# A graph network's GATv2 layer: its feed-forward node work moved from a phase of its own into the edge sweep, with logits and scatter in column parts

## The reference

```
h  = relu(layernorm(x))
xl = h @ W_l + b_l ; xr = h @ W_r + b_r ; ee = edge_attr @ W_e
m  = leaky_relu(xl[src] + xr[dst] + ee, 0.2)          # one row of 128 per edge
logits = einsum('eho,ho->eh', m, att)                 # 8 per edge
ex = exp(logits - segment_max(logits, dst)[dst])
out = segment_sum(xl[src] * ex / segment_sum(ex)[dst], dst) + b_att
hh  = layernorm(out + h) * g1 + be1
ff  = gelu(hh @ W1 + b1) @ W2 + b2                    # 128 -> 512 -> 128
x   = x + layernorm(hh + ff) * g2 + be2
```

## Time and profile before

| what | value |
|---|---|
| time, median of three runs | 7462.92 us |
| span of the profiled execution | 5796.6 us |
| profiled execution's own time | none is given beside the span; median less span is 1666.3 us |
| GATv2 sweep, first to last gather | 2282.0 to 3349.9 us |
| FFN phase, first operation to the next sweep's first gather | 3407.5 to 3621.1 us |
| PE, DVE, ACT, POOL busy over the span | 79%, 47%, 21%, 69% |

### The profile page before, as it was taken

One profiled execution on the slowest core, in us unless ns is written; L12 is line 12 of the kernel. 1 busy time (PEld: TensorE's weight loads), 2 busy tenths in 40 slices (PEclk: granted clock), 3 DMA queues, 4 the chain that ended last, 5 costly groups with the idle time before them and its releaser, 6 DMA issues. The chain is left out here.

```text
span 5796.6 us, 89863 instructions
## 1 busy us (share of the span) xinstructions
PE 4596.1 (79%) x21959; PEld 3153.3 (54%) x21959; DVE 2702.8 (47%) x8105; ACT 1216.6 (21%) x3182; POOL 3988.9 (69%) x4207
## 2 busy tenths in 40 slices
PE   5888888657777776999999977687777758887887
PEld 4777777535556564444444433455555535555555
DVE  4222222321111113677777766555555545555555
ACT  2111111221211211222222258111111111111111
POOL 6777777457777775777777700777777747777775
PEclk9999999975555555999999989666666666666665
DMA  5333333244444443555555510455555534444443
GB/s 151 106 105 105 105 104 104 74 150 106 112 114 107 118 114 90 160 165 165 165 165 164 166 38 24 109 114 114 113 114 115 113 77 107 111 109 110 109 111 78
DMA packets 559823, 663.58 MB, mean 114 GB/s; under 512 B 196431, under 2 KB 390909, under 8 KB 558717
## 3 DMA queue, kind: packets, MB, share of 16 engines
q1 hardware_dynamic: 424909, 382.99, 22.2%
q0 software_dynamic: 134640, 277.80, 21.1%
HBM read 580.95 MB, written 86.19 MB: 115 GB/s over the span
## 5 line engine op out<-in xcount | busy, mean ns | idle before, releaser
L1792 POOL DMA_INDIRECT soft_rows<-table,sources x2496 | 2388.6, 957 | 1128.2 <-issue 737.7
L1422 POOL DMA_INDIRECT sum_rows<-table,sources x832 | 785.7, 944 | 343.9 <-issue 249.6
L1088 POOL DMA_INDIRECT term_rows<-table,sources x832 | 791.4, 951 | 289.4 <-issue 289.4
L1923 PE MATMUL psum<-soft_onehot,soft_message 128*128 128x64 f32 x3328 | 647.6, 358 | 107.1 <-DVE soft_message L2066 105.0
L1923 PEld LDWEIGHTS psum<-soft_onehot,soft_message 128*128 128x128 f32 x3328 | 586.1, 266 | 188.0 <-issue 181.8
L1119 PE MATMUL psum<-term_onehot,term_term 128*128 128x64 f32 x1664 | 403.9, 425 | 188.5 <-DVE sums L1171 176.6
L1464 PE MATMUL psum<-sum_onehot,sum_rows 128*128 128x64 f32 x1664 | 360.4, 391 | 222.7 <-DMA sum_rows<-table,sources 218.4
L1119 PEld LDWEIGHTS psum<-term_onehot,term_term 128*128 128x128 f32 x1664 | 370.7, 328 | 242.1 <-issue 242.0
L1165 DVE TENSOR_TENSOR term_term<-psum,term_rows 128x512 f32<-128x512 f32 x208 | 143.9, 692 | 753.0 <-issue 349.0
L1464 PEld LDWEIGHTS psum<-sum_onehot,sum_rows 128*128 128x128 f32 x1664 | 343.5, 304 | 278.0 <-issue 273.8
L1919 PEld LDWEIGHTS psum<-soft_onehot,soft_weights 128*4 128x4 f32 (+1 forms) x3328 | 284.9, 109 | 305.9 <-issue 293.0
(11 more groups left out here) (277 smaller groups left out, 6619.9 us busy)
## 6 DMA issues: line engine op xcount, KB each, us to landing
soft_onehotT<-onehotsT SPq DMA_DIRECT2D x312, 256.0 KB
soft_onehot<-onehots SPq DMA_DIRECT2D x624, 128.0 KB, 2.1
soft_attrs<-in_ea128T SPq DMA_DIRECT2D x208, 256.0 KB
soft_rows<-table,sources POOLq DMA_INDIRECT x2496
term_attrs<-in_ea64T SPq DMA_DIRECT2D x208, 128.0 KB, 2.8
onehots<-term_onehot SPq DMA_DIRECT2D x208, 128.0 KB
sum_onehot<-onehots SPq DMA_DIRECT2D x208, 128.0 KB, 2.7
onehotsT<-sum_flat SPq DMA_DIRECT2D x208, 128.0 KB
```

The source lines that it names most:

```text
L1088: pool.indirect_dma_start(rows[:, k, t, :], None, io.table0[0:NCH * CN], bass.IndirectOffsetOnAxis(sb.sources[:, g * TPG + t:g * TPG + t + ...
L1422: pool.indirect_dma_start(rows[:, k, t, :], None, io.table1[0:NCH * CN], bass.IndirectOffsetOnAxis(sb.sources[:, g * TPG + t:g * TPG + t + ...
L1792: pool.indirect_dma_start(rows[:, k, t, :], None, table[0:NCH * CN], bass.IndirectOffsetOnAxis(sb.sources[:, g * TPG + t:g * TPG + t + 1], ...
L1923: last = pe.matmul(bank[:, 0:W], message[:, g.slot(4), b, :], onehot[:, k, b], start=b == 0, stop=b == TPG - 1)
```

## The change

The order of phases becomes first phase, two sweeps with their norms, `gatv2_sweep`, `soft_sweep(3)`, `soft_sweep(4)`; `ffn_phase` is no longer called and `soft_sweep` loses its `full` branches. In `gatv2_sweep`:

- The FFN work (`FfnNodes`, with three `ChunkNorm`) runs inside the sweep in chunks of 256 nodes. It has one PSUM bank (bank 4), which each stage takes over when the one before it is read. Stages are placed by offsets from 2 to 24. The gain and bias of the first norm are applied on ACT in feature-major form. Many of its tiles lie in SBUF of weights that are no longer needed.
- Logits: a whole batch at once at the start of a step, with one attention matrix `att_cols` (128 x 32). Four matmuls write 32 lanes each, on four column quarters of one bank of 128 lanes. The lanes of a batch now fill 128 partitions instead of 32, in one bank instead of two.
- Scatter: the tiles of a group go alternately to rows 0 to 63 and 64 to 127 of the window bank. `flip_window` follows directly and is a matmul with `fold` (two identities on top of each other), which adds the two parts. The weights' transposes become matmuls with `quad_pick`.
- `z` has four buffers instead of two; the starts and continuation masks of a batch are loaded with four DMAs each instead of one.
- 64 steps are unrolled ahead of the loop instead of 16, and the sweep runs on to step 248, where the last chunk is stored.
- The first phase loads five more small constants.

```diff
@@ class FfnNodes: stages (new) @@
+    def act_steps(self, act, t):
+        node_steps(act, t, (2, self.stage), (4, self.norm1.take_root), (6, self.normalise1), (7, self.scaled1), (8, self.gelus(0)), (9, self.gelus(1)),
+                   (12, self.copy_res), (13, self.norm2.take_root), (14, self.normalise2), (19, self.norm3.take_root), (20, self.normalise3),
+                   (21, self.copy_h), (22, self.rows_out))
...
+    def attention(self, v, c, t):
...
+        v.tensor_scalar(self.den, self.dens, 1e-16, None, ALU.add).then_inc(s.den[k], 1)
...
+        v.tensor_tensor(heads, heads, self.den.unsqueeze(3).broadcast_to([P, CB, 8, D // 8]), ALU.mult).then_inc(s.ratio[k], 1)
...
+        self.norm1.statistics(v, c, kept)
@@ def gatv2_sweep: PE (new) @@
+                def head_logits(g):
+                    pe.wait_ge(s.leaky, g.times(1, BATCH))
+                    if g.back(BATCH).exists():
+                        pe.wait_ge(s.factor_log, g.back(BATCH).uses(BATCH))
+                    settle(pe)
+                    for j in range(BATCH):
+                        last = pe.matmul(lane_bank[j * QUAD:(j + 1) * QUAD], sb.att_cols, z[:, j], start=True, stop=True)
...
+                    for b in range(TPG):
+                        last = pe.matmul(window_bank[b % 2 * W:b % 2 * W + W], onehot[:, k, b], message[:, g.slot(2), b, :], start=b < 2, stop=b >= TPG - 2)
...
+                def flip_window(g):
+                    pe.wait_ge(s.window_copied, g.times(1, 1))
...
+                    pe.matmul(window_T[:, 0:W], window[:, 0:D], fold, start=True, stop=True)
...
+                def step(t):
+                    if t.back(BATCH).closes(0):
+                        head_logits(t.back(BATCH))
+                    if t.exists():
+                        edge_terms(t)
+                    nodes.pe_steps(pe, t)
...
+                    g = t.back(LAG)
+                    if g.exists():
+                        scatter(g)
+                        flip_window(g)
@@ def gatv2_sweep: DVE (new) @@
+                def step(t):
+                    g = t.back(1)
+                    if g.exists():
+                        v.wait_ge(s.z, g.times(1, 1))
+                        v.scalar_tensor_tensor(z[:, g.slot(BATCH)], z[:, g.slot(BATCH)], 0.2, z[:, g.slot(BATCH)], ALU.mult, ALU.max).then_inc(s.leaky, 1)
...
+                    if t.exists():
+                        edge_sum(t)
+                    nodes.dve_steps(v, t)
```

More of the change, by code:

```diff
@@ L42 @@
 BATCH = 4
+QUAD = P // BATCH
 LAG = BATCH + 3
@@ L1651, in soft_sweep @@
 def soft_sweep(nc, io, sb, layer):
-    H = {2: 8, 3: 4, 4: 1}[layer]
+    H = {3: 4, 4: 1}[layer]
     L, W = H * BATCH, NARROW
[L1655 to L1658, removed]
+    table, width = {3: (io.table3, D + 4), 4: (io.table4, D + 1)}[layer]
+    dst_table, dst_width = {3: (io.adst3, 4), 4: (io.adst4, 2)}[layer]
@@ L1659, in soft_sweep @@
+    spread = {3: sb.lane_expand4, 4: sb.ones}[layer]
     mask, heads = sb.lane_mask[0:L], sb.lane_head[0:L, 0:H]
     AHEAD = 4
-    DST = AHEAD if full else BATCH
     phase = f"soft{layer}"
[L1663 to L1667, removed]
@@ L1668, in soft_sweep @@
-    s = sems(nc, phase, *names, gathered=AROUND, attr=AHEAD, dst_rows=DST, onehotT=4, onehot=4)
+    FIRST = 4 * AROUND
+    LAST = STEPS * (NCH - 1 + BEHIND) + 14
+    names = ("order cleared starts_in cont_in edge_term leaky src_out logits lanes_out running backward fend carry_psum carry shift init_psum init maxima "
+             "shifted factor_log weights_lane factor spread weights_T weights_out factor_psum factor_out message "
+             "scattered").split()
+    s = sems(nc, phase, *names, gathered=AROUND, dst_rows=BATCH, onehotT=4, onehot=4)
@@ L1711, in soft_sweep @@
         factor_head_bank = sb.psum[0:H, 7, 48:48 + BATCH]
-        nodes = None if full else GatNodes(nc, io, sb, tile, layer, sb.psum[:, 2, :])
-        CLEARED = 4 + (not full)
+        nodes = GatNodes(nc, io, sb, tile, layer, sb.psum[:, 2, :])
+        CLEARED = 5
         ORDER = 4
@@ L1809, in step @@
                 def step(t):
-                    if not full and t.back(BATCH).closes(0):
+                    if t.back(BATCH).closes(0):
                         take_sources(t.back(BATCH))
@@ L1846, in step @@
                     if g.closes(0):
-                        act.wait_ge(s.logits, g.times(1, BATCH) if full else g.uses(BATCH))
+                        act.wait_ge(s.logits, g.uses(BATCH))
                         if g.back(BATCH).exists():
@@ L1899, in src_logits @@
                     last.then_inc(s.logits, 1)
-                def scatter(g):
-                    k = g.slot(4)
-                    wait_past(pe, s.window_copied, g, 1, 0)
-                    pe.wait_ge(s.onehot[k], g.uses(4, 16))
-                    pe.wait_ge(s.columns, g.times(1, 1))
-                    pe.wait_ge(s.message, g.times(1, 1))
-                    for b in range(TPG):
-                        last = pe.matmul(window_bank, onehot[:, k, b], message[:, g.slot(2), b, :], start=b == 0, stop=b == TPG - 1)
-                    last.then_inc(s.scattered, 1)
                 def scatter_T(g):
@@ L1942, in step @@
                     if g.exists():
[L1943 to L1946 removed]
+                        scatter_T(g)
+                    if t.back(BATCH).closes(0):
                         src_logits(t.back(BATCH))
[L1948 to L1949 removed]
                     g = t.back(BATCH + 1)
@@ L2071, in step @@
                 def step(t):
-                    g = t.back(1)
-                    if g.exists() and full:
-                        v.wait_ge(s.z, g.times(1, 1))
-                        v.scalar_tensor_tensor(z[:, g.slot(2)], z[:, g.slot(2)], 0.2, z[:, g.slot(2)], ALU.mult, ALU.max).then_inc(s.leaky, 1)
                     g = t.back(LAG)
```

708 lines of the change are left out of this document (584 added, 124 removed).

## The result

The changed kernel took 7522.4 us (median of four runs, 7515.9 to 7547.3) against 7464.6 for the kernel before: slower by a ratio of 1.008, 95% interval 1.0055 to 1.0105.

The account below looks back on a forecast made before the run. PE was taken to bound the GATv2 sweep. FFN phase -214, steps without nodes +8, batches with nodes +296, drain +57, setup +1 sum to +148; 7463 + 148 = 7611, with a little for SP 7615 us, range 7540 to 7690.

Parts of the forecast that it names:

- Outside the span lie 1666.3 us that no row explains; I carry them over unchanged.: Whole run: time beyond the profile's span of 5796.6 us, added unchanged to the forecast.
- the sum: Whole kernel: FFN phase -214, steps without nodes +8, batches with nodes +296, drain +57, setup +1, giving +148 us.
- The clock: Rival, GATv2 sweep: TensorE's granted clock falls, halving for half the sweep; some +300 us on top, 7950; chance 0.07.
- PE clock 1.00: Sign that the forecast is right: PE keeps a granted clock of 1.00; below 0.9 would show it wrong.
- its batch: GATv2 sweep: a batch with nodes takes 27.6 us against 20.8 before, +6.8, times 43.5 batches: +296 us.
- Column parts: Rival, logits and scatter: parts run wholly side by side, 1.7 us less per batch, -88 us, 7530; chance 0.10.
- The waits: PE's waits per batch with nodes: window 4 × 0.5, exponential 1.5, leaky relu 2.1; 5.6 of 27.6 us.
- the loop's turn: GATv2 sweep: the turn of the loop adds 0.7 us per eight steps with nodes.
- The table load: Exponential's wait 1.5 instead of 0.87 us through a 1.28 us load; a 1.38 us drain would add about 60 us.
- The drain: GATv2 sweep's end: remaining scatters and last node chunks take 88 us instead of 31, +57; bounds +15 and +90.
- Waits hidden: Rival, GATv2 sweep: queue or engine slack absorbs PE's three waits, 22.0 us per batch remain, 7360 us; chance 0.29.

Follow-up runs that it names:

- the pair with the extra copy: Kernel before and changed kernel, each with one more 1 MB DRAM to DRAM copy per group in the GATv2 sweep: before 6638 us, changed 6571 us.
- the version without nodes: Changed kernel with FFN work taken out of the sweep and the old FFN phase behind it: 5987 us; with idle matmuls in PE's waits 5790 us.
- the first pair: Kernel before and changed kernel, unmodified, as first timed where transfers land late: 7464.6 and 7522.4 us, ratio 1.008.

## Why the prediction was wrong, point by point

The steps can be read off PE's timeline of the changed kernel, profiled again under the condition of the rows of before:

```profile
3018.35 0.38 PE L2141 MATMUL psum<-ones,soft_shift 8*128 8x1 f32 x2
3018.65 0.68 PE L2121 MATMUL psum<-soft_message,soft_onehot 128*64 128x136 f32 x8
3019.91 0.41 PE L2128 MATMUL psum<-L_W,soft_window 128*128 128x64 f32 x2 [0.57 <-ACT soft_window L2068]
3020.24 0.28 PE L2129 MATMUL psum<-L_W,soft_window 128*8 128x64 f32 x2
3021.76 1.05 PE L2159 MATMUL psum<-quad_pick,soft_lanes 128*128 128x32 f32 x8 [1.24 <-ACT soft_lanes L2078]
3022.64 0.42 PE L2163 MATMUL psum<-soft_factors,quad_expand 128*128 128x4 f32 x2
3023.00 0.20 PE L2164 MATMUL psum<-soft_factors,quad_head 128*8 128x4 f32 x2
3023.13 1.11 PE L2096 MATMUL psum<-ident,soft_rows 128*128 128x128 f32 x4
3024.04 1.91 PE L2102 MATMUL psum<-soft_attrs,L_We 128*128 128x512 f32 x2
3025.88 1.27 PE L2103 MATMUL psum<-soft_onehotT,rel_group 64*128 64x512 f32 x2
3027.08 0.44 PE L1771 MATMUL psum<-ident,L_blr 128*128 128x128 f32 x2
3027.46 0.68 PE L2121 MATMUL psum<-soft_message,soft_onehot 128*64 128x136 f32 x8
3028.62 0.41 PE L2128 MATMUL psum<-L_W,soft_window 128*128 128x64 f32 x2 [0.47 <-ACT soft_window L2068]
3028.95 0.28 PE L2129 MATMUL psum<-L_W,soft_window 128*8 128x64 f32 x2
3031.18 1.06 PE L2111 MATMUL psum<-soft_z,att_cols 128*32 128x512 f32 x8 [1.95 <-DVE soft_z L2267]
3032.18 0.66 PE L2096 MATMUL psum<-ident,soft_rows 128*128 128x128 f32 x4
3032.67 1.02 PE L2102 MATMUL psum<-soft_attrs,L_We 128*128 128x512 f32 x2
...
3050.96 1.05 PE L2159 MATMUL psum<-quad_pick,soft_lanes 128*128 128x32 f32 x8 [1.23 <-ACT soft_lanes L2078]
```

and ACT's:

```profile
3019.39 0.28 ACT L2068 ACTIVATE soft_window<-psum 128x136 f32<-128x136 f32 x1 [0.45 <-PE psum L2121]
3019.69 1.28 ACT L2078 ACT_TABLE_LOAD   x1
3020.98 0.63 ACT L2078 ACTIVATE soft_lanes<-soft_lanes 128x512 f32<-128x512 f32 x1
```

- **The step that failed first: "Outside the span lie 1666.3 us that no row explains; I carry them over unchanged."** Nothing lies outside the span (5804.4 of 5807 us in the kernel before, 7526.0 of 7528 in the changed one). The changed kernel takes 1382 us more where transfers land late, all of it inside the span, and most of it in phases that the change does not touch; for the kernel before the same is inferred. The change then costs +58 instead of +340. That its extra time hid behind waits for transfers is the best reading, by the estimate of +433 against +157 above and by the pair with the extra copy, whose difference is -67; no profile of before under late transfers shows it. The unexplained fifth of the time was the main finding of the page, and the sum should have had a case for it.
- **The clock** is the step that failed under the condition of the rows, where +148 was forecast and +340 measured: "PE clock 1.00". Its fall was a rival with a chance of 0.07 and a price of +300. In the rows above the edge features (L2102) take 1.91 us behind the wait of 1.24 and 1.02 two steps later; over the sweep the clock is 0.82. Filling the waits takes 197 us away in the version without nodes, more than its 188, and with the logits moved as well 272 of the 340. The prediction laid its batch out at full clock, 27.6 us. The one in the rows above takes 29.2 (3021.76 to 3050.96), but it is one of the short ones: over 32 batches the weights' matmuls (L2159) come every 31.9 us:

```profile
2737.26 1.05 PE L2159 MATMUL psum<-quad_pick,soft_lanes 128*128 128x32 f32 x8 [1.20 <-ACT soft_lanes L2078]
3757.82 1.05 PE L2159 MATMUL psum<-quad_pick,soft_lanes 128*128 128x32 f32 x8 [1.23 <-ACT soft_lanes L2078]
```

  With the clock held and the logits late it is 26.3 (the same over 28 batches, 2776.02 to 3513.56), against 20.9 before.
- **Column parts** run wholly side by side, the rival with 0.10: four logits matmuls take 1.00 us (3031.18 to 3032.18) where one took 0.98, forecast 2.27; the scatter is recorded with 0.68 against 1.14. The Trainium skill states in "TensorE: Matmul & The Clock Gate", part on packing small matmuls, that matmuls on different column tiles run at once; this case agrees, with four in the time of one where the page has 2.38 times the rate for three. By the prediction's own working that is 1.7 us per batch, 88 in all, which the sum should have had as a gain. That this rival's time, 7530, lies 8 us from the measured 7522 is luck: it holds neither the fall of the clock nor the late transfers, and these cancel nearly.
- **The waits were sized well:** for the window 0.57 and 0.47 (forecast 0.5), for the exponential 1.24 (1.5), for the leaky relu 1.95 and, a batch later, 2.03 (2.1). All waits of PE come to 210 us in 1100, 6.1 per batch, where 5.6 were laid out. Missed was the loop's turn on DVE. Once in 16 steps the leaky relu starts late without waiting for anything that the profile shows, and the logits then wait 4.98 us:

```profile
3091.36 0.69 DVE L2267 SCALAR_TENSOR_TENSOR soft_z<-soft_z 128x512 f32<-128x512 f32 x1 [2.82 <-issue]
```

  The kernel before has the same gap (2.3 to 2.6 us), but there a batch with it takes only 1.3 us more; here it takes 36.2 (3079.85 to 3116.09) instead of some 29. The sum had 0.7 for every eight steps.
- **The table load** is 1.28 and the exponential starts 1.29 after it: no drain behind it here either, against the rule of the Trainium skill ("ScalarE: Activation LUTs", section on what ACT_TABLE_LOAD costs) that the prediction weighed.
- **The drain** was sized nearly right. The forecast was -214 and +57, that is -157, and from the last gather it is only -101, but most of that gap belongs to the sweep. PE's last full step ends at 3859, 68 us behind the last gather, where it was 26 before. From that step to the next sweep's first gather it is 101 us, against 88 laid out; the last FFN products run at half speed there (L1788 2.05 us instead of 1.13). Counted to PE's last full step, the sweep has grown by 482 us, against 304 forecast, or 216 with the column parts' gain.
- **"Waits hidden"** (0.29, below before) did not happen where transfers are quick. Under the extra copy the kernel came out below before, by transfers and not by DVE's slack.

## What to carry to other kernels

Check that the profile's span is the time you are to explain before you build a sum on it; if not, the waits that matter may not be in the rows. On a stage that PE bounds at full clock, count each new wait twice: for its length, and for the slower matmuls behind it; work that fills the waits, even idle work, took 197 and 135 us off here, while moving real work into them (the destination product, the nodes' stages) gained less, because another consumer then waited. Judge an edit in the condition that it will run in: this one costs 5.8% where transfers are quick, 0.8% where they land late, and gains 1% where an added copy keeps the DMA engines full.

## What the runs showed of the hardware

Some 200 waits of at most 0.8 us each on PE, 116 of 1000 us in all, went with a mean granted clock of 0.80 where the kernel before had 1.00; two and four idle 128x128x128 matmuls ahead of them brought it back to 1.00, and 197 us with it. Four 32-column f32 matmuls with different column quarters as targets take as long as one (1.00 against 0.98 us), and a scatter in two 64-column parts 0.61 from start to start (version with column parts in the kernel before) instead of 1.07. A table load on ACT took 1.28 us, with no drain ahead of the next ACTIVATE. The changed kernel took 6140 or 7522 us, and the kernel before 5800 or 7463, with nearly equal durations of each gather (944 and 947 ns); in the slower profile the engines waited for transfers to land, with the DMA engines only 0.30 to 0.39 busy in the sweeps. Why they landed late stays open: the chip of the first pair is not known, and no run tried another cause than the added copy, which fills the DMA engines as the first pair did not.
